# A gated graph network of five layers on one core: the first units' work in another order, shift on GpSimd, the last mask in PSUM

## What is computed

```python
h = jnp.maximum(_layernorm(x, axis=-1), 0.0)
A = (adj != 0).astype(x.dtype)
for l in range(5):
    m = jnp.einsum('bnd,de->bne', h, weight[l])
    agg = jnp.einsum('bij,bid->bjd', A, m)
    gi = agg @ w_ih.T + b_ih;  gh = h @ w_hh.T + b_hh
    r = sigmoid(i_r + h_r);  z = sigmoid(i_z + h_z)
    n = tanh(i_n + r * h_n)
    h = (1.0 - z) * n + z * h
x = x + h * mask[..., None]
```

## Time and profile before

| | |
|---|---|
| Time, median of 3 runs | 384.85 us (384.82 to 385.16) |
| Profiled execution: own time | 386.38 us |
| its span | 384.4 us |
| mean granted clock of PE | 0.989 |
| PE busy | 367.2 us, 96% |
| DVE, ACT, GpSimd busy | 80%, 77%, 71% |
| HBM read, written | 17.57 MB, 4.19 MB |

### The profile page before, as it was taken

One profiled execution on the slowest core, in us unless ns is written; L12 is line 12 of the kernel. 1 busy time (PEld: TensorE's weight loads), 2 busy tenths in 40 slices (PEclk: granted clock), 3 DMA queues, 4 the chain that ended last, 5 costly groups with the idle time before them and its releaser, 6 DMA issues.

```text
span 384.4 us, 6567 instructions
## 1 busy us (share of the span) xinstructions
PE 367.2 (96%) x2182; PEld 188.7 (49%) x2182; DVE 308.0 (80%) x568; ACT 295.0 (77%) x489; POOL 273.8 (71%) x245
## 2 busy tenths in 40 slices
PE   5867999999999999999999999999999999999992
PEld 2433555555555555555555555555545555555541
DVE  5676788888887778888888898877777778777776
ACT  3587789889978777888898977788776777677662
POOL 4456677887897678777769595947876655544796
PEclk9899999999999999999999999999999999999997
DMA  8733346396573645444366664306633342298422
GB/s 239 171 55 82 84 114 125 66 210 112 131 180 82 97 96 113 107 113 82 83 90 148 98 151 121 107 10 158 136 84 84 88 77 56 57 183 214 97 82 82
DMA packets 107793, 42.89 MB, mean 112 GB/s; under 512 B 84833, under 2 KB 101473, under 8 KB 107761
## 3 DMA queue, kind: packets, MB, share of 16 engines
q1 hardware_dynamic: 107232, 41.76, 49.5%
q10 hardware_dynamic: 432, 0.66, 0.6%
q0 software_dynamic: 96, 0.07, 0.1%
HBM read 17.57 MB, written 4.19 MB: 57 GB/s over the span
## 4 chain that ended last, share of the span: by engine, by line
PE 89%; DVE 4%; DMA 3%; ACT 1%; issue 1%; POOL 1%; DVEq 0%; POOLq 0%
PE ps_r L250 9%; PE ps_r L251 9%; PE ps_z L251 9%; PE ps_z L252 9%; PE ps_r L252 9%; PE ps_z L250 9%; PE ps_s L309 4%; PE ps_s L308 4%; PE ps_in L252 4%; PE ps_hn L251 4%; PE ps_in L251 4%; PE ps_hn L250 4%; PE ps_in L250 4%; PE ps_hn L252 4%; PE ps_t L317 2%; DMA hp<-nat 2%
## 5 line engine op out<-in xcount | busy, mean ns | idle before, releaser
L698 POOL TENSOR_TENSOR zh<-z,h 128x512 f32<-128x512 f32 x80 | 101.5, 1269 | 85.8 <-ACT z L411 85.4
L405 ACT ACTIVATE r<-ps_r,b_sum,unscale 128x512 f32<-128x512 f32 x80 | 62.2, 777 | 56.7 <-PE ps_r L252 54.9
L531 DVE SCALAR_TENSOR_TENSOR rhn<-ps_hn,b_hn,r 128x512 f32<-128x512 f32 x80 | 60.0, 750 | 26.2 <-ACT r L405 26.1
L703 POOL TENSOR_TENSOR hp<-h,hp 128x512 f16<-128x512 f32 x64 | 74.0, 1156 | 0.0
L537 DVE TENSOR_TENSOR ps_in<-ps_in,rhn 128x512 f32<-128x512 f32 x80 | 55.9, 699 | 19.6 <-PE ps_in L252 18.3
L416 ACT ACTIVATE ps_in<-ps_in,b_ih,unscale 128x512 f32<-128x512 f32 x79 | 59.2, 750 | 13.1 <-DVE ps_in L537 11.2
L543 DVE SCALAR_TENSOR_TENSOR ps_in<-z,ps_in 128x512 f32<-128x512 f32 x79 | 54.6, 691 | 10.4 <-ACT ps_in L416 10.4
L411 ACT ACTIVATE z<-ps_z,b_sum,unscale 128x512 f32<-128x512 f32 x80 | 61.5, 769 | 0.7 <-PE ps_z L252 0.7
L548 DVE TENSOR_TENSOR h<-zh,ps_in 128x512 f32<-128x512 f32 x78 | 53.6, 687 | 8.7 <-POOL zh L698 0.8
L525 DVE TENSOR_TENSOR s_lo<-ps_s,s_hi 128x512 f16<-128x512 f32 x80 | 54.4, 680 | 1.4 <-ACT s_hi L399 1.4
L399 ACT CAST s_hi<-ps_s 128x512 f16<-128x512 f32 x80 | 46.6, 583 | 2.6 <-PE ps_s L309 1.4
(11 more groups left out here) (88 smaller groups left out, 745.9 us busy)
## 6 DMA issues: line engine op xcount, KB each, us to landing
x_in<-in_x SPq DMA_DIRECT2D x16, 256.0 KB, 4.6
adj_in<-in_adj SPq DMA_DIRECT2D x16, 256.0 KB, 4.1
x_out<-in_xT SPq DMA_DIRECT2D x16, 256.0 KB, 3.2
mask_in<-in_mask_row SPq DMA_DIRECT2D x16, 256.0 KB, 3.9
out<-x_out SPq DMA_DIRECT2D x15, 256.0 KB, 2.3
nat<-hp SPq DMA_TRANSPOSE x64, 3.1
fold_in<-in_fold_lhs SPq DMA_DIRECT2D x1, 320.0 KB, 4.8
out<-x_out ACTq DMA_DIRECT2D x1, 256.0 KB, 2.3
```

Source lines behind the costliest of these rows:

```text
L405: nc.scalar.activation(r[:], ps_r[:], ACT.Sigmoid, bias=b_sum[:, 0:1], scale=unscale[:, 0:1]).then_inc(r_done, 1)
L531: nc.vector.scalar_tensor_tensor(out=rhn[:], in0=ps_hn[:], scalar=b_hn[:, 0:1], in1=r[:], op0=ALU.add, op1=ALU.mult).then_inc(rhn_done, 1)
L698: nc.gpsimd.tensor_tensor(zh[:, K % 2], z[:, K % 2], h[:, t % RING], ALU.mult).then_inc(zh_done, 1)
L703: nc.gpsimd.tensor_tensor(h_lo(t), h[:, t % RING], h_hi(t), ALU.subtract).then_inc(h_lo_done, 1)
```

## The change

1. **Loads.** `whh_sb` and `wih_sb` are issued by SP behind the load of tile 0's x, ahead of `fold_in`; ACT issues no load any more.
2. **Shift.** DVE negates the mean right behind the aggregates (`minus_mean`, new tile), and GpSimd multiplies it by rstd at the end of `inverse_std`. `shift_of` on DVE is gone, for all 16 tiles.
3. **Blank products.** 24 instead of 18 ahead of the bound's product, 4 instead of 8 behind the first fold.
4. **Unit 0 in three passes.** `first_h_products` makes all high-by-high products, then all high-by-low, then all low-by-high, and waits for the low parts only ahead of the second and third pass.
5. **Order.** On ACT, `natural_high(1)` moves ahead of `v_high(0)` and `s_high(0)`, `transposed(0)` behind them, and tile 2's `layernorm` out of unit 0 into the opening. On DVE, `moments(2)` moves ahead of the first adjacency. On PE, tile 1's transpose moves from before unit 0's s products to behind its r and z products.
6. **Last unit.** After the last gate r ACT copies the mask of the last tile to ps_s; DVE reads it there and writes (z - 1)*mask over `mask_in`; tanh is written in place in PSUM and no longer to r.

```diff
@@ sync @@
             load_x(0)
+            sp.dma_start(whh_sb[:], w_hhT).then_inc(whh_loaded, 16)
+            sp.dma_start(wih_sb[:], w_ihT).then_inc(wih_loaded, 16)
             sp.dma_start(fold_in[:].rearrange("p (l d) -> p l d", l=L), fold_lhs).then_inc(fold_loaded, 16)
@@ tensor @@
+            def first_h_products():
+                banks = (ps_r, ps_z, ps_hn)
+                pe.wait_ge(h_hi_init, 1)
+                pe.wait_ge(u_hi_done, 1)
+                for k, ps in enumerate(banks):
+                    nc.tensor.matmul(ps[:], block_of(u_hi, k), h_hi(0), start=True, stop=False)
+                pe.wait_ge(h_lo_init, 1)
+                for k, ps in enumerate(banks):
+                    nc.tensor.matmul(ps[:], block_of(u_hi, k), h_lo(0), start=False, stop=False)
+                pe.wait_ge(u_lo_done, 1)
+                for k, ps in enumerate(banks):
+                    nc.tensor.matmul(ps[:], block_of(u_lo, k), h_hi(0), start=False, stop=k == 2)
...
-                awake(18)
+                awake(24)
...
-                awake(8)
+                awake(4)
                 pe.wait_ge(top_done, 1)
-                pe.wait_ge(u_lo_done, 1)
...
                 if K == 0:
                     aggregate(0)
-                    transpose_first(1)
...
-                if 2 <= K + 1 < FIRST:
+                if K + 1 < FIRST:
                     transpose_first(K + 1)
@@ scalar @@
+            def move_mask():
+                f = (TILES - 1) % FRING
+                act.wait_ge(ends_loaded[f], 32 * ((TILES - 1) // FRING + 1))
+                act.wait_ge(s_lo_done, N)
+                nc.scalar.copy(ps_s[:], mask_in[:, f]).then_inc(mask_moved, 1)
...
             def first():
-                act.dma_start(whh_sb[:], w_hhT).then_inc(whh_loaded, 16)
-                act.dma_start(wih_sb[:], w_ihT).then_inc(wih_loaded, 16)
...
                 natural_high(0)
-                transposed(0)
                 layernorm(1, 0)
                 layernorm(1, 1)
+                natural_high(1)
                 v_high(0)
                 s_high(0)
-                natural_high(1)
+                transposed(0)
+                layernorm(2, 0)
+                layernorm(2, 1)
...
                     gate_r(K)
+                    move_mask()
...
-                if K < FIRST - 2:
+                if 0 < K < FIRST - 2:
                     layernorm(K + 2, 0)
                 gate_n(K)
...
+                if 0 < K < FIRST - 2:
+                    layernorm(K + 2, 1)
                 if K < FIRST - 2:
-                    layernorm(K + 2, 1)
                     natural_high(K + 2)
@@ vector @@
                 last.then_inc(aggr_done, 1)
+                dve.wait_ge(aggr_done, t + 1)
+                nc.vector.tensor_scalar(minus_mean[:, t % 2], mean_var[:, t % 2, :, 0], -1.0, None,
+                                        ALU.mult).then_inc(minus_done, 1)
...
-                nc.vector.scalar_tensor_tensor(out=ps_s[:], in0=z[:, K % 2], scalar=1.0, in1=mask_in[:, f],
+                dve.wait_ge(mask_moved, 1)
+                nc.vector.scalar_tensor_tensor(out=mask_in[:, f], in0=z[:, K % 2], scalar=1.0, in1=ps_s[:],
                                                op0=ALU.subtract, op1=ALU.mult).then_inc(open_done, 1)
...
-                nc.vector.tensor_tensor(ps_in[K % 2][:], ps_s[:], r[:], ALU.mult).then_inc(zn_done, 1)
+                nc.vector.tensor_tensor(ps_in[K % 2][:], mask_in[:, f], ps_in[K % 2][:], ALU.mult).then_inc(zn_done, 1)
@@ gpsimd @@
                 if t >= 2:
-                    pool.wait_ge(shift_done, t - 1)
                     pool.wait_ge(h0_done, 2 * (t - 1))
...
+                pool.wait_ge(minus_done, t + 1)
+                pool.wait_ge(rstd_done, t + 1)
+                nc.gpsimd.tensor_tensor(shift[:, t % 2], minus_mean[:, t % 2], rstd[:, t % 2], ALU.mult).then_inc(shift_done, 1)
```

More of the change, by code:

```diff
@@ L112, in gnn_kernel @@
         rstd = sb("rstd", [P, 2, TG])
+        minus_mean = sb("minus_mean", [P, 2, TG])
         shift = sb("shift", [P, 2, TG])
@@ L338, in first @@
                 fold(0)
-                awake(8)
+                awake(4)
                 pe.wait_ge(top_done, 1)
-                pe.wait_ge(u_lo_done, 1)
             first()
             for K in range(N):
-                h_products(K)
+                if K:
+                    h_products(K)
+                else:
+                    first_h_products()
                 if K == N - 1:
@@ L414, in gate_n @@
                 act.wait_ge(npre_done, K + 1)
-                n = ps_in[K % 2] if K < N - 1 else r
-                nc.scalar.activation(n[:], ps_in[K % 2][:], ACT.Tanh, bias=b_ih[:, 2:3],
+                nc.scalar.activation(ps_in[K % 2][:], ps_in[K % 2][:], ACT.Tanh, bias=b_ih[:, 2:3],
                                      scale=unscale[:, 0:1]).then_inc(n_done, 1)
@@ L422, in state_high, with u_high @@
                 nc.scalar.copy(h_hi(t), h[:, t % RING]).then_inc(h_hi_done, 1)
+            def u_high():
+                act.wait_ge(whh_loaded, 16)
+                act.wait_ge(scale_done, 1)
+                nc.scalar.activation(u_hi[:], whh_sb[:], ACT.Copy, scale=scale[:, 0:1]).then_inc(u_hi_done, 1)
             def v_high(l):
@@ L441, in first @@
                 transposed_high(0)
-                act.wait_ge(whh_loaded, 16)
-                act.wait_ge(scale_done, 1)
-                nc.scalar.activation(u_hi[:], whh_sb[:], ACT.Copy, scale=scale[:, 0:1]).then_inc(u_hi_done, 1)
+                u_high()
                 natural_high(0)
-                transposed(0)
                 layernorm(1, 0)
                 layernorm(1, 1)
+                natural_high(1)
                 v_high(0)
                 s_high(0)
-                natural_high(1)
-                if DIRECT > 1:
-                    transposed_high(1)
+                transposed(0)
+                layernorm(2, 0)
+                layernorm(2, 1)
                 act.wait_ge(bias_done, 2)
@@ L508, in first_adjacency @@
                 nc.vector.tensor_scalar(a[:, t], adj_in[:, t], 0.0, None, ALU.not_equal).then_inc(a_done, 1)
-            def shift_of(t):
-                dve.wait_ge(rstd_done, t + 1)
-                if t >= 2:
-                    dve.wait_ge(h0_done, 2 * (t - 1))
-                nc.vector.scalar_tensor_tensor(out=shift[:, t % 2], in0=mean_var[:, t % 2, :, 0], scalar=-1.0,
-                                               in1=rstd[:, t % 2], op0=ALU.mult, op1=ALU.mult).then_inc(shift_done, 1)
             def transposed_low(t):
```

30 lines of the change are left out of this document (10 added, 20 removed).

## The result

The changed kernel takes **382.2 us** (median of 9 executions, 381.56 to 383.89), the kernel before beside it 384.82 (384.72 to 386.43): ratio 0.9925, 95% interval 0.9909 to 0.9942. The gain is 2.6 us where 5.5 were forecast, and 382.2 lies outside the range of 378.2 to 381.6. The profiled execution of the changed kernel took 382.2, its span 380.2.

What follows compares the result with a forecast made beforehand. The kernel's length was taken as tile 3's transpose landing, plus a PE stream that does not wait, plus the tail. Gains 4.8 + 0.7 = 5.5 gave 384.85 - 5.5 = 379.4 us; 8-in-10 range 378.2 to 381.6.

Steps and rivals of the forecast that it cites:

- the one ahead of Part 1: Baseline step: durations from one profiled execution (own time 386.38), their differences subtracted from the unprofiled median of 384.85.
- Part 1: Opening loads: x0 lands 0.8 us earlier, at 3.93; no wait for `fold_in` counted, bound 0.3; one queue costs 0.1.
- Part 3: PE's opening, blanks and three passes: clock kept, first real product at 10.7, nine products end at 12.65 instead of 16.21.
- Part 5: Tail: masked operation takes 0.69 instead of 1.57 us, product starts at 379.30 instead of 380.03; gain 0.7, bounds 0 and 0.8.
- Part 2: Shift on GpSimd: first layernorm 0.96 us earlier, 0.16 of it from the shift; added operations cost nothing in the long stretch.
- Part 4: ACT's and GpSimd's order, units 0 to 3: tile 3's transpose lands at 31.6 instead of 36.54, 4.9; less queue 0.1, 4.8.
- The clock under the real products: Rival, 8%: clock falls at 10.7 under unit 0's real products, s_mm 2.3 late; time 381.4.
- Slower: Rival, 4%: GpSimd late in the long stretch, 0.55 us on each of 12 later tiles, 6.6 lost; time 386.0.
- Given back: Rival, 6%: DVE's small operations block against GpSimd twice, or load queue holds first transposes; half of last 3 us lost: 382.3.

Runs made afterwards that it cites:

- Experiment 1: The kernel before, rerun unchanged: 384.92 us, ratio 0.9992; executions fall into two groups.
- experiment 12: No new kernel: `fold_in` landings read in five profiled executions (changed kernel, old PE opening, blanks in PE's idle pieces); own times 381.56 to 383.07 us.
- experiment 13: Changed kernel with six blank products behind unit 0's aggregation and four behind unit 0's last products: 382.35 us, ratio 0.9936.
- experiment 2: Changed kernel with the loads of `whh_sb` and `wih_sb` back on ACT's queue: 382.13 us, ratio 0.9923.
- experiment 4: Changed kernel with `fold_in` issued by ACT, written behind the first sigmoid: 382.55 us, ratio 0.9942.
- experiment 5: Changed kernel with `fold_in` issued by ACT, written ahead of the first sigmoid: 382.51 us, ratio 0.9936.
- experiment 6: Kernel before with only the last-unit (tail) change: 384.38 us, ratio 0.9997; group against group 384.30 against 384.78.
- experiment 14: Kernel before with shift on GpSimd and new tail: 383.3 us; with the new order too: 383.87, four of 12 executions at 382.21 to 382.57.
- experiment 7: Kernel before with only the shift change (`minus_mean` on DVE, product with rstd on GpSimd): 383.69 us, ratio 0.9965.
- experiment 9: Changed kernel with the old order of ACT, DVE and PE, three sets: 382.21, 383.09 and 382.71 us; all 19 executions have median 382.67.
- after_again: Changed kernel rerun unchanged: 383.2 us (7 executions), ratio 0.9937; its profiled execution took 381.56.

## Why the prediction was wrong

**Direction and mechanism were right in the main.** In the first profile tile 3's transpose set the time, PE had no listed wait past unit 3's first product, shift takes 0.20 on GpSimd, the masked operation 0.68. The size was wrong by 2.8 us (382.2 against 379.4), in four places.

**The step that failed most is the one ahead of Part 1: "I take differences in that trace from the median."** The trace had an own time of 386.38 and the median was 384.85, and I said so without asking what the 1.5 us were. Part 3 then counted the lost clock (the first real product at 14.27, eight blanks in 3.42 us) as something to be won, and took it from a median that had never paid it. Experiment 1 shows that: the traced execution near the median starts the first real product at 12.55 and unit 3 at 35.06. The same steps against the trace's own time give 386.38 - 5.5 = 380.9. That is 1.5 of the 2.8.

**Part 1, `fold_in`: "DVE wants it only at 6.2 ... I count no wait, with 0.3 as a bound".** It landed at 7.64 and DVE waited 1.7 us. I took its flight for the same "with about as many bytes ahead of it", although it was issued 1.0 us later and behind both weights on the one queue. Unit 1 started at 19.79 instead of 18.9, unit 3 at 32.56 instead of 31.65. That is 0.9 of the 2.8. The table of experiment 12 says the same from another side: in those executions the end is 374.6 us behind its landing. No run had both x at 3.5 and `fold_in` ahead of 6.9, so what an early `fold_in` would have given is not shown. The blanks might have been in the way then: the prediction had the 24 end at 7.84, from a trace in which they turned fast early, and they ended at 8.57 in the first profile, at 9.39 in that of experiment 13. The gain of Part 1 (x 0.8 earlier, in fact 1.2) was real and reached the layernorm, but not the bound's product, and experiments 2, 4 and 5 show that it was worth nothing in the end.

**Part 5: "it ends at 379.06 ... 0.7".** DVE's chain did get 0.76 shorter, but the last store took 0.3 longer beside the one of tile 14. Worth 0.5 (experiments 6 and 14). The forecast ended the tail at the product and did not follow it to the landing: 0.2.

**Part 2: "in the long stretch beside a PE that never waits: nothing there".** From unit 3's first product to the last matmul PE took 340.6 us (373.17 - 32.56), where it had taken 340.3 (376.91 - 36.59). The traces divide by the place of the shift alone (experiment 7). One `minus_mean` of the long stretch took 1.18 us instead of the 0.15 counted, and a product of PE behind it came 0.22 us late. That is 0.3. With it the 2.8 is accounted for: 1.5 + 0.9 + 0.2 + 0.3 = 2.9, less the 0.1 that Part 4 had put aside.

**Part 2 was undersized, Part 4 oversized.** The prediction gave the shift 0.16 by itself and laid out the rest of the 4.8 as order. One by one they are: the shift 1.2, the tail 0.5, blanks and passes and loads nothing that can be told. The order is not settled: 1.0 in four chosen executions (experiment 14), 0.1 at full clock with a late `fold_in` (experiment 9), and in the medians 382.67 against 382.21 over different chips, but 382.71 against 383.2 the other way round on the one chip that ran both. 384.8 - 1.2 - 0.5 - 1.0 = 382.1 closes the sum only with the first of these. Part 4's own times for unit 1 (18.9) and unit 3 (31.65) are each 0.9 early, which is `fold_in` carried through. Unit 2 is 2.1 early (24.5 against 26.63): beside the 0.9, tile 2's transpose, issued at 22.26, flew 4.3 us where the layout took 3.14 (in the trace before it had flown 3.6). This was off the chain by 0.34 us only, PE's last wait.

**Rivals.** The clock under the real products, at 8%, may have been underrated: 5 of 21 executions of the changed kernel have the lower mean clock and a time 1.0 us or more above the median, and in the old order the fall is seen at 20 us. Part 3's reason against it, that gaps of up to 2.15 us left the clock alone, does not carry over: there it fell behind 1.89. It doesn't explain the median. The Trainium skill (TensorE: Matmul & The Clock Gate, "Part 4: PE-mode transpose") says that transposes do not count as PE activity. In all three traces of the changed kernel the granted clock stayed at 1.00 around the four transposes at 8.6 to 9.3 us, which does not tell whether they count. *Slower* was right in kind, 0.3 us where it had 6.6: a small operation was held, once, and it was DVE's. *Given back* gave 382.3, the measured time, but by another mechanism than small operations blocked on DVE. It was in the main the entry of the chain, not its middle.

## What to carry to other kernels

Before costs are taken from a trace, hold its own time against the median of the runs; if they differ by more than the effect sought, find the rows that make the difference, and count nothing as gain that the median doesn't pay. Where an early consumer needs the last of several loads, the earliest load is worth nothing by itself; move all of them or none. A small operation given to another engine can cost time far behind the stage that it was meant for: compare the long stretch too, to 0.1 us. And follow a tail to the landing of its last store.

## What the runs showed of the hardware

**One queue moved less than two, for a while, in the traces of this kernel.** With the same loads in the changed kernel, the weights on ACT's queue (experiment 2) or on SP's (as changed), the stretch of 4 to 5 us reads, for experiment 2:

```profile
4.00:5.00 1.00, 1.00 (x4) 0.30 (x3) 0.15 (x1) 0.00 (x0) 0.00 (x0) 1.00 1.01 387
```

So 387 GB/s against 197. From 2 to 3 us it is the other way round (157 against 291), and from 6 to 8 us it is 286 against 325. Over 2 to 8 us together two queues moved 1.78 MB, one 1.71 (1.66 and 1.79 in the other two traces of the changed kernel). The Trainium skill (DMA: Bandwidth & Descriptors, "Issuing engines are not separate DMA queues") says that a second issuing engine saves only issue time. The rate of a single microsecond does not agree with that; the sum and the time (382.1 to 382.2 for both kernels) do not speak against it. The rate on one queue also differs between executions (265 in the same stretch of `after_again`), and `fold_in`'s flight is 4.7 to 6.2 us there.

**Early products run at half pace for a time that varies** while the granted clock already reads 1.00 (experiment 1): 18 blanks lasted 5.36 or 6.99 us, 24 lasted 7.11 to 8.21. How many blanks bridge a gap depends on it. So one program has two times, 1.5 us apart.

**Some DVE operations are held by a GpSimd one beside them, some are not.** The 128x4 shift took 1.12 us, and when it had gone, the adjacency in its place took 1.38 instead of 0.41; `minus_mean` took 1.18 instead of 0.17. The moments of a tile took their usual 0.87 beside the same kind of subtraction (12.00, changed kernel).

**A transposing DMA's flight varies.** Tile 1's took 3.1 or 3.2 us in the traces, tile 2's 3.0 to 4.7 in the changed kernel and its variants (4.3 and 4.7 by the same program). Why is not shown.
